# First attention of a two-layer transformer kernel: three products as split fp32r pairs, softmax sums from a column of ones, keys and queries in alternate steps

## The reference, cut to what matters

```python
mod = silu(c) @ ada_w.T + ada_b                 # shift, scale, gate per sequence
h = layernorm(x) * (1 + scale_msa) + shift_msa
q, k, v = split(h @ qkv_w.T + qkv_b)            # 16 heads of 16 features
attn = softmax(where(mask, q @ k.T * 16 ** -0.5, -1e9))
x = x + gate_msa * ((attn @ v) @ proj_w.T + proj_b)
```

## Time and profile before

| | us |
|---|---|
| median of 3 runs | 2631.7 (2631.47 to 2634.01) |
| profiled execution | 2632.17 |
| its span | 2630.1 |
| TensorE busy | 2432.8 (92%) |
| VectorE busy | 1954.8 (74%) |
| ScalarE busy | 1544.7 (59%) |
| GpSimd busy | 1034.6 (39%) |

### The profile page before, as it was taken

One profiled execution on the slowest core, in us unless ns is written; L12 is line 12 of the kernel. 1 busy time (PEld: TensorE's weight loads), 2 busy tenths in 40 slices (PEclk: granted clock), 3 DMA queues, 4 the chain that ended last, 5 costly groups with the idle time before them and its releaser, 6 DMA issues. The chain is left out here.

```text
span 2630.1 us, 68444 instructions
## 1 busy us (share of the span) xinstructions
PE 2432.8 (92%) x25680; PEld 2106.9 (80%) x25680; DVE 1954.8 (74%) x3768; ACT 1544.7 (59%) x2913; POOL 1034.6 (39%) x872
## 2 busy tenths in 40 slices
PE   5999999969999988999999999999999924999997
PEld 4777777749999977888888888888888823899996
DVE  4888888856666757888888888888888867666663
ACT  3777777746666645555555555555555643655653
POOL 1676777730000013443443344334433402355544
PEclk8999999969999998999999999999999956999998
DMA  4111111100101110000000000000000021244332
GB/s 122 30 32 34 34 32 32 32 25 23 31 20 30 30 51 11 15 16 16 12 16 16 16 12 16 16 16 12 16 16 16 13 61 42 81 93 91 84 64 32
DMA packets 86352, 89.22 MB, mean 34 GB/s; under 512 B 26752, under 2 KB 80640, under 8 KB 83584
## 3 DMA queue, kind: packets, MB, share of 16 engines
q1 hardware_dynamic: 73984, 71.10, 8.9%
q0 software_dynamic: 12288, 17.05, 4.0%
HBM read 62.42 MB, written 25.69 MB: 34 GB/s over the span
## 5 line engine op out<-in xcount | busy, mean ns | idle before, releaser
L975 POOL TENSOR_TENSOR a_rq<-a_vq,minus_half 128x8 f32<-128x8 f32 x256 | 417.4, 1640 | 104.0 <-DVE a_vq L1000 104.0
L928 ACT ACTIVATE a_sq<-a_bqk 128x512 f32<-128x512 f32 x256 | 152.1, 594 | 312.8 <-PE a_bqk L126 312.8
L970 POOL TENSOR_TENSOR a_rstd<-a_veps,minus_half 128x1 f32<-128x1 f32 x64 | 35.3, 552 | 626.7 <-DVE a_veps L1044 626.7
L124 PE MATMUL a_bqk<-wqk_hi,a_h_lo 128*128 128x512 f32 x512 | 206.5, 403 | 5.1 <-DVE a_h_lo L1016 5.1
L126 PE MATMUL a_bqk<-wqk_hi,a_h_hi 128*128 128x512 f32 x512 | 201.1, 393 | 0.0
L125 PE MATMUL a_bqk<-wqk_lo,a_h_hi 128*128 128x512 f32 x512 | 200.9, 392 | 0.0
L992 DVE TENSOR_TENSOR a_qk<-a_bqk,a_rq 128x512 f32<-128x512 f32 x256 | 175.7, 687 | 29.9 <-POOL a_rq L975 29.7
L1729 DVE TENSOR_TENSOR e_u_lo<-e_u,e_u_hi 128x512 fp32r<-128x512 f32 x128 | 88.9, 695 | 126.9 <-ACT e_u_hi L1592 126.2
L920 ACT COPY a_vs<-a_ba 64x512 f32<-64x512 f32 x256 | 149.0, 582 | 53.6 <-PE a_ba L126 48.9
L1587 ACT ACTIVATE e_u<-e_bu,e_b 128x512 f32<-128x512 f32 x128 | 88.3, 690 | 156.8 <-PE e_bu L126 154.9
L440 POOL TENSOR_TENSOR a_kbd<-a_kT,consts_sb 128x512 f32<-128x512 f32 x128 | 130.9, 1044 | 125.7 <-PE a_bs L565 122.4
(11 more groups left out here) (259 smaller groups left out, 7826.9 us busy)
## 6 DMA issues: line engine op xcount, KB each, us to landing
X<-in_x SPq DMA_DIRECT2D x64, 128.0 KB, 2.1
a_gate<-gates_of_rows SPq DMA_DIRECT2D x128, 64.0 KB, 2.5
m_gate<-gates_of_rows SPq DMA_DIRECT2D x32, 256.0 KB, 4.2
tokens<-a_xs SPq DMA_DIRECT2D x64, 128.0 KB, 1.7
out<-a_xs SPq DMA_DIRECT2D x64, 128.0 KB, 1.7
e_w<-in_fc1s SPq DMA_DIRECT2D x8, 1024.0 KB, 5.0
e_w<-in_fc2s SPq DMA_DIRECT2D x8, 1024.0 KB, 4.8
a_w<-in_fc_w SPq DMA_DIRECT2D x2, 1024.0 KB, 6.1
```

What stands on the lines that cost most here:

```text
L124: tensor.matmul(to, w_lo, x_hi, start=start, stop=False)
L928: nc.scalar.activation(sq[:, n * BK:(n + 1) * BK], b_qk[:, n * BK:(n + 1) * BK], ACT.Square).then_inc(s["sq"], 1)
L975: nc.gpsimd.tensor_tensor(rq[:, 8 * n:8 * n + 8], vq[:, 8 * n:8 * n + 8], g.mhalf[:, 0:8], ALU.pow).then_inc(s["rq"], 1)
```

## The change

In the first attention:
- The qkv and projection weights are split into fp32r parts at the start of the stage (ScalarE, VectorE, GpSimd). The high and low parts of qkv lie in the buffer that later takes the MLP's parts; the MLP's second weight is loaded where the plain weights were, once they are split.
- Tokens are split too: VectorE casts `hT` to `h_hi`, GpSimd makes `h_lo`. Outputs: ScalarE casts to `o_hi` instead of its copy, VectorE makes `o_lo` straight from PSUM.
- Keys, queries, values and the projection become fp32r in three products. Keys are made in even steps, queries in odd ones, each for two tiles at once (256 columns). Values are made with tokens as output rows, 256 columns, and copied by four ScalarE copies instead of two.
- Each head in `vm` has a 17th column of ones, so the product with the probabilities also gives their sums. VectorE's sum goes; the reciprocal reads the sums from PSUM.
- The offsets change: moments +5, power +5, normalizing +4, transposition +3, token parts +2, value copies −1, spread keys −1, scores −2, exponential −3, transposed probabilities −4 (through one bank, in two halves), times values −5, output and projection −6, update −7. The order within a step is new on every engine. SP loads 14 tiles ahead. The update works in one buffer instead of two.

The core of the diff, the new side of TensorE's step (`T2` = 256, `HV` = 17):

```diff
@@ setup_phase, GpSimd
+                for r in range(2):
+                    pool.wait_ge(cleared, r + 2)
+                    at = r * (HD0 + 1) + HD0
+                    nc.gpsimd.memset(g.vm[r * S:(r + 1) * S, :, :, :, at:at + 1], 1.0).then_inc(cleared, 1)
@@ attention0_phase, SyncE
-                AHEAD = 8
+                AHEAD = 14
...
+                sp.wait_ge(s["own_lo"], 2)
+                sp.wait_ge(s["vb_mm"], 1)
                 sp.dma_start(w2[:, :, :], a["fc2_0_w"]).then_inc(s["w_in"], 16)
@@ attention0_phase, TensorE
+                    def turn_probs(n):
+                        for k in range(4):
+                            j = 4 * n + k
+                            last = nc.tensor.transpose(
+                                b_pt[:, k * P:(k + 1) * P],
+                                pr[:, turn % VB, 2 * j:2 * j + 2, :].rearrange("p h k -> p (h k)"), ident)
+                        last.then_inc(s["pT"], 1)
+                    def product(to, off, done):
+                        for n in range(DC):
+                            cols = slice((off + n) * P, (off + n + 1) * P)
                             for kc in range(DC):
+                                last = split_sum(nc.tensor, to[:, n * T2:(n + 1) * T2], wqkv_hi[:, kc, cols],
+                                                 wqkv_lo[:, kc, cols], h_hi[:, pair, kc, :], h_lo[:, pair, kc, :],
+                                                 n == 0 and kc == 0, kc == DC - 1)
+                        last.then_inc(s[done], 2)
                     if has(-4):
+                        pe.wait_ge(s["exped"], i - 3)
+                        if has(-5):
+                            pe.wait_ge(s["pT_out"], 2 * (i - 4))
+                        turn_probs(0)
+                    if has(-6):
+                        pe.wait_ge(s["normed"], i - 5)
...
                         last.then_inc(s["oT"], 1)
+                    if has(-5):
...
+                        pe.wait_ge(s["pT_out"], 2 * (i - 4))
+                        for j in range(H // 2):
                             for b in range(2):
+                                last = nc.tensor.matmul(b_o[toks, 2 * j * HV:2 * (j + 1) * HV],
+                                                        PT[:, (turn - 5) % 2, j, toks],
+                                                        g.vm[:, (turn - 5) % VB, b, j, :], start=True, stop=True)
+                        last.then_inc(s["o"], 1)
+                    if has(-4):
+                        pe.wait_ge(s["pT_out"], 2 * (i - 4) + 1)
+                        turn_probs(1)
+                    if has(0) and turn % 2 == 0:
+                        pe.wait_ge(s["h_lo"], i + 2)
+                        if has(-2):
+                            pe.wait_ge(s["k_out"], i)
+                        product(b_k, DC, "k")
+                    if has(0) and turn % 2 == 1:
+                        if has(-2):
+                            pe.wait_ge(s["q_out"], i - 1)
+                        product(b_q, 0, "q")
+                    if has(3):
+                        pe.wait_ge(s["xhat"], i + 4)
+                        if has(-1):
+                            pe.wait_ge(s["vm"], i)
...
                         last.then_inc(s["xT"], 1)
                     if has(-2):
+                        pe.wait_ge(s["kbd"], i - 1)
+                        pe.wait_ge(s["q_out"], i - 1)
+                        if has(-3):
+                            pe.wait_ge(s["scored"], i - 2)
...
                         last.then_inc(s["s"], 1)
+                    if has(-6):
+                        pe.wait_ge(s["o_lo"], i - 5)
                         for kc in range(DC):
+                            last = split_product(nc.tensor, b_pj[:, 0:D], o_hi[:, kc, :], o_lo[:, kc, :],
+                                                 wp_hi[:, kc, :], wp_lo[:, kc, :], kc == 0, kc == DC - 1)
                         last.then_inc(s["proj"], 1)
+                    if has(0):
+                        if has(3):
+                            pe.wait_ge(s["hT"], i + 4)
...
+                            last = split_product(nc.tensor, b_vx[:, 0:D], h_hi[:, pair, kc, toks], h_lo[:, pair, kc, toks],
+                                                 wqkv_hi[:, kc, 2 * D:3 * D], wqkv_lo[:, kc, 2 * D:3 * D],
+                                                 kc == 0, kc == DC - 1)
+                        last.then_inc(s["v"], 1)
```

```diff
@@ attention0_phase, GpSimd
+                        pool.wait_ge(s["h_hi"], i + 3)
+                        nc.gpsimd.tensor_tensor(h_lo[:, pair, :, at], hT[:, :, at], h_hi[:, pair, :, at].bitcast(F32),
+                                                ALU.subtract).then_inc(s["h_lo"], 1)
...
+                        pool.wait_ge(s["eps"], i + 6)
...
+                        pool.wait_ge(s["k_out"], i)
+                        if has(-2):
+                            pool.wait_ge(s["s"], i - 1)
```

More of the change, by code:

```diff
@@ L306, in attention0_phase @@
-        vbB = m.sb("a0_vbB", [P, DC, P])
+        vbB = o_sb[:, :].rearrange("p (c q) -> p c q", c=DC)
         pbB = m.sb("a0_pbB", [P, D])
-        b_qk, b_vt = m.ps("a0_bqk", 4 * P), m.ps("a0_bvt", 4 * P)
-        VB = 4
+        b_q, b_k, b_vx = (m.ps("a0_b" + n, 4 * P) for n in ("q", "k", "vx"))
         b_s = m.ps("a0_bs", H * S)
[L311 to L315, removed]
+        b_pt = m.ps("a0_bpt", 4 * P)
@@ L359, in step @@
[L359 to L396, removed]
@@ L417, in step @@
                 def step(i, has, turn):
[L418 to L425, removed]
-                        if isinstance(i, int) and i == 5:
+                    if has(-7):
+                        pool.wait_ge(s["proj_out"], i - 6)
+                        if later(i - 7):
+                            pool.wait_ge(s["res"], i - 7)
+                        if isinstance(i, int) and i == 7:
@@ L481, in step @@
[L481 to L484 removed]
+                    pa = pr[:, (turn - 2) % VB, :, :]
+                    if has(-6):
+                        dve.wait_ge(s["o_hi"], i - 5)
+                        nc.vector.tensor_tensor(o_lo[:, :, :], b_pj[:, D:2 * D].rearrange("p (c q) -> p c q", c=DC),
+                                                o_hi[:, :, :].bitcast(F32), ALU.subtract).then_inc(s["o_lo"], 1)
@@ new lines, in step @@
+                    if has(3):
+                        pe.wait_ge(s["xhat"], i + 4)
+                        if has(-1):
+                            pe.wait_ge(s["vm"], i)
+                        elif later(i + 3):
+                            pe.wait_ge(s["hT"], i + 3)
+                        for c in range(DC):
+                            last = nc.tensor.transpose(b_vx[:, D + c * P:D + (c + 1) * P],
+                                                       xhat[(turn + 3) % 2][:, c * P:(c + 1) * P], ident)
+                        last.then_inc(s["xT"], 1)
@@ L577, in step @@
-                    if has(-3):
-                        if later(i - 3):
-                            pe.wait_ge(s["normed"], i - 3)
-                        for j in range(H // 2):
-                            if j % 4 == 0:
-                                pe.wait_ge(s["pT_out"], 2 * (i - 3) + j // 4 + 1)
-                            for b in range(2):
-                                toks = slice(b * S, (b + 1) * S)
-                                last = nc.tensor.matmul(b_o[toks, 2 * j * HD0:2 * (j + 1) * HD0],
-                                                        PT[:, (turn - 3) % 2, j, toks],
-                                                        g.vm[:, (turn - 3) % VB, b, j, :], start=True, stop=True)
-                        last.then_inc(s["o"], 1)
```

295 lines of the change are left out of this document (166 added, 129 removed).

## The result

The changed kernel takes **2564.0 us** (median of 4 runs, 2563.53 to 2564.41) where the kernel before, timed beside it, takes 2632.9 (2631.47 to 2635.14): a ratio of 0.9745, 95% interval 0.9734 to 0.9757. The prediction was 2567 us.

The account below looks back on a forecast made before the run. TensorE's instruction stream was taken as the first attention's bound: 61 x 1.14 = 69.5 us saved, less 4.5 for head and tail, is 65; from 2632.17 that gives 2567.2, the median 0.5 lower: 2567 us, range 2554 to 2598.

Parts of the forecast that it names:

- TensorE's own step: TensorE's work for one 128-token tile in the first attention: 6.77 us predicted, 1.14 below 7.91.
- What was left at 2.79: TensorE's transposes of outputs, probabilities and normalized tokens, and the scores: predicted to stay at 2.79 us a step.
- the 7.91: Time of one step in the kernel before, 7.91 us over 61 steps of the first attention, taken as bound by TensorE.
- the eight groups follow each other without a wait: Reading of TensorE's step in the kernel before: no waits between its groups of operations within 7.90 us.
- about 6.1 us: VectorE's predicted time a step in the first attention, 5.9 us busy plus waits, under TensorE's 6.77.
- The 1.68 us of idleness: GpSimd's wait a step before the spread keys in the kernel before; predicted to be gone.
- one update stretched to about 1.5 us: Sign expected in the new profile: one of GpSimd's residual updates, 0.73 us undisturbed, lasting about 1.5 us.
- The walk: Walk through one step: VectorE's shift falls on GpSimd's first updates, costs about 0.8 us; GpSimd's round 6.7, under 6.77.
- the first rival: GpSimd and VectorE become the first attention's bound through their shared port: 6.9 to 7.37 us a step; chance 0.20.
- Rival 2: ScalarE's four value copies delay the modulated tokens for the values product, up to 0.3 us a step, 2585; chance 0.06.
- Rivals 3 and 4: 3: GpSimd still idles before spread keys, 2707 us, chance 0.03; 4: fp32r products no faster, about 2636, chance 0.02.
- Head and tail: Start and end of the first attention: predicted to cost 1.5 us and 3 us, 4.5 together.

Follow-up runs that it names:

- The first experiment: Cast of the tokens to their high part moved from VectorE to ScalarE, against the changed kernel: 2573.5 us, ratio 0.9776 to the kernel before.

## Why the prediction was right, and where it was not

**TensorE's own step** was forecast at 6.77 us and is 6.78 to 6.79 where the others don't hold it. Queries and keys 1.52 (forecast 1.44: their first product takes 0.21 instead of 0.12), values 0.72 (0.72), projection 0.81 (0.72, the same 0.2 at its start; the values, right behind it, have none), probabilities times values 1.06 (1.10, almost at the lower bound). What was left at 2.79 is 6.78 − 4.11 = 2.67. The excesses, 0.17, and the savings, 0.16, cancel, which was luck.

**What the 7.91 was made of** I had wrong in one term. "Queries and keys 306.59 − 304.52 = 2.07" and "the eight groups follow each other without a wait" took 0.29 us of waiting for VectorE for product time. The sum did not suffer, since the new price of these products came from elsewhere; the reason did. With the runs, the 68 us split so: 37 by the new order, lags and the ones column with plain products of 128 columns (2631.9 to 2594.6, among it 0.29 a step of waiting and 0.16 for values in wide products), some 6 by their width, 24 by fp32r. Of the 37, no run tells order from lags. This split depends on the order in which the parts are taken: with 128 columns fp32r costs 50 us (2594.6 to 2644.6) instead of giving 24.

**VectorE** was forecast with its cast at 0.29; it is 0.77, because the cast meets GpSimd at the port as well. That made VectorE full (47.06 of 50) and not "about 6.1 us".

**GpSimd.** The 1.68 us of idleness went as forecast, the low part costs 0.74 (0.73), and "one update stretched to about 1.5 us" is 1.72. The walk gave a round of 6.7 us under TensorE's 6.77, with 0.8 us of stalls by the port; the stalls are (1.72 − 0.73) + (0.88 − 0.73) = 1.14, and the round is 6.85, above TensorE's. So what bounds the steady state is the mechanism of the first rival, below that rival's own 6.9 to 7.37: 0.05 us a step, 3 us in all: the runs with less work for GpSimd (2560.4) and with less for TensorE (2562.9) show both sides of that. The prediction named the right mechanism, took it for hidden and put its round 0.15 us too low.

**ScalarE.** Four value copies cost 4 x 0.266 = 1.06 us, forecast 1.1; keys or queries cost 0.87 where "about 0.7" was taken. Rival 2 did not come. **Rivals 3 and 4** did not come either: no idle time before the spread keys, and a pace of 0.12 us.

**Head and tail.** The first product was expected some 5 us later and came 4.75 later. The tail was mis-sized: from the last scores to the last update it is 504.98 − 478.41 = 26.57 us against 572.06 − 546.27 = 25.79, 0.8 more where I took 3. Steps at both ends of the loop are shorter too: once GpSimd makes no more low parts, scores follow each other at 455.47, 461.85 and 468.23, 6.38 us apart; in these steps TensorE turns no tokens either. In all, 61 x (7.91 − 6.83) = 65.9 us, and the stage gained 67.1: head and tail gave 1.2 instead of costing the 4.5. That is 5.7 better than forecast, and the step 0.06 x 61 = 3.7 worse: the two errors of the sum nearly cancel, by luck, and leave 2.0 us; the 1.4 gained outside the stage, which no term had, come on top. So it is 2567 against 2564.

## What to carry to other kernels

Here split products paid only where each weight load was followed by 256 columns and not 128: three fp32r products of 256 columns took 0.36 us against 0.43 for a plain one, and three of 128 columns 0.33 against 0.22. A timeline of matmuls without gaps is no proof that TensorE does not wait: look at the waits of its weight loads, and hold a group's duration against the same instructions elsewhere. And when an operation goes to GpSimd, count what VectorE does through the shared port in the same round, casts and normalizations of fp32 too: here each engine waited for the other's whole instructions, and taking one collision away can put another in its place.

## What the runs showed that I had not expected

A cast of 128x256 to fp32r waits for GpSimd to end (0.77 us against 0.28 to 0.29 where GpSimd was idle or only began), and so does a normalization that reads one fp32 tile and two columns of scalars (0.79 and 0.80 against 0.40). GpSimd's power of a single column is held as well: 2.00 us in the head, under VectorE's 1.75 us subtraction, against 0.54.

An fp32r product with fresh 128x128 weights was passed every 0.11 us with 128 columns and every 0.12 us with 256, at the granted clock of 1.00. Which of its parts sets the 0.11 was not tried.

The first experiment stays as a warning: work taken off the engine that looked full (with the cast gone, VectorE's busy time fell from 47.06 to 46.78 of 50 us only, because the stalls came back) cost 9.5 us.
